# Attention block on one Trainium2 core: the first five and the last four tiles over two sets of buffers

## The chip, the cores and the metric

The kernel runs on one core of a Trainium2 chip. The core has TensorE (matrix products, its clock granted at one of two levels, 1.2 or 2.4 GHz), VectorE, ScalarE, GpSimd and SyncE, which here only issues DMAs. Each engine works through its own instruction list in order, and they meet through semaphores. The metric is the device time of one execution in microseconds; lower is better.

## The reference

An input `x` of 8 x 512 x 512 goes through three residual layers: half of an expert layer, a differential attention, and the expert layer again. Cut to what matters:

```python
x = x + 0.5 * ffn(layernorm(x))      # phase 1
x = x + attn(layernorm(x))           # phase 2
x = x + 0.5 * ffn(layernorm(x))      # norm and expert product: phase 2, the choice: phase 3

def attn(x):                         # S = E = 512, H = 16, KVH = 4, D = 32
    q, k, v = x @ Wq, x @ Wk, x @ Wv          # 2*H*D, 2*KVH*D, KVH*D columns
    q, k = rope(q), rope(k)                   # k, v repeated over 4 heads
    scores = softmax(causal(q @ k.T) / sqrt(D))        # two maps for each head
    diff = softmax(causal(scores[0] - lam * scores[1]))
    att = rmsnorm(diff @ v) * rms_w * (1 - LAM_INIT)
    return att @ Wo

def ffn(x):                          # 16 experts with the same weight, 256 tokens each
    S = softmax(x @ router_w + router_b)
    G, idx = top_k(S.T, 256)
    return scatter_add(idx, G * (x[idx] @ expert_w + expert_b))
```

## The kernel before

The 4096 rows are 32 tiles (`NT`) of 128 rows, four (`TB`) to a batch. Phase 1 (to about 188 us) writes the first layer's result `x1` to DRAM. Phase 2 is the attention with the norm and the expert product behind it. Phase 3 (from 1858.74 us) chooses tokens and adds the output.

In phase 2 a tile passes three steps. **Preparation**: load `xs`, `stats` and `normalise`, a split in a high and a low fp16 half (`high`, `low`), the turning of both (`turn_x`) and its copy to `xt` (`take_x`), three products with `wqkv` into PSUM (`project(0..2)`, 12 matmuls each), `rope` on VectorE, `rope_add` and `rope_low` on GpSimd, `rope_high` on ScalarE, a second turning (`turn_chunks`) and its copies to `turned` (`take_chunks`). SyncE then spreads `turned` into `qs` and `ks` with 12 + 12 DMAs (`stack`). **Attention**: eight pairs of query tiles and heads for each of the 32 steps `K`. **After-work**: squares and sums of each head, a root on GpSimd (`head_root`), norm, split, turning, product with `wo` (`product_o`), the sum with `x1`, norm, root (`root2`), split, turning, the router's product, the expert's product (`expert`, 13 matmuls), and the store of `x2` and `y2`.

`run_bodies` writes each engine's list. Inside `body` a table of 24 slots says which step of preparation (for tile K + 5, `AHEAD`) and of after-work (for tile K - 5, `BEHIND`) stands beside which step of attention. Five tiles must be prepared before step 0, and four tiles (28 to 31) are left after the last body; nothing of attention runs beside these. They run in two loops, one over `alone` and one over `closing`:

```python
    with eng.Fori(0, AHEAD) as tau:
        for f, next_tile in alone:
            f(tau + 1 if next_tile else tau)
```

In these loops each buffer exists once (`xs`, `rot`, `scratch`, `split`, `turned`; `an`, `at`, `x2`, `post_bank`), apart from some more PSUM banks in the first (`spread[0]`) and one other buffer in the second. SyncE's part of the first loop is

```python
                with sp.Fori(1, AHEAD) as u:
                    load(u + 1)
                    stack(u, None)
```

so the load of tile u + 1 stands behind the 24 DMAs of the stack of tile u - 1, which waits for that tile's last copy. The first product of attention, `energies`, waits for `turned_out` of tile 4 and for the stacks of tiles 0 to 3 to have landed. Below, the stretch from 188 us to that product is called the opening, the stretch from the last `weigh` to the first load of phase 3 the closing.

Of the kernel before, what the change touches and what calls it, by code (L numbers as in the profile page):

```python
# [15 lines left out]
ALU = mybir.AluOpType  # L16
# [7 lines left out]
ds = bass.ds  # L24
# [16 lines left out]
STEPS = 8  # L41
NC = (NQ + NK) // P
# [102 lines left out]
def run_bodies(eng, attention, side, ahead, alone, spread, closing):  # L145
# [10 lines left out]
    def body(K, tau, pi, pairs=True, more=True):  # L156
        known = {}
        for j in range(STEPS):
            for i in range(3):
# [4 lines left out]
                for f in side.get(3 * j + i, ()):  # L164
                    f(tau, pi)
# [4 lines left out]
    for slot in sorted(ahead):  # L170
        for f in ahead[slot]:
            f(0)
# [13 lines left out]
    body(NT, None, NT - BEHIND)  # L186
    spread[1] = True
    for f, next_tile in closing:
        if next_tile:
            f(NT - BEHIND + 1)  # L190
    with eng.Fori(NT - BEHIND + 1, NT - 1) as pi:
        for f, next_tile in closing:
            f(pi + 1 if next_tile else pi)
    for f, next_tile in closing:
        if not next_tile:
            f(NT - 1)
    spread[1] = False


def program(nc, x, wqkv, wo, we, wr, lams, rms, rb, eb, consts, out, x1_d, x2_d, y2_d):  # L200
# [14 lines left out]
    with top:  # L215
# [709 lines left out]
        with ExitStack() as ctx:  # L925
# [31 lines left out]
            ast = sb2("ast", [P, 4, H])  # L957
            an = sb2("an", [P, E])
# [9 lines left out]
            spread = [False, False]  # L968

            def project_bank(n):  # L970
                return bank[:, (4, 5, 0)[n] if spread[0] else 4, :]

            def chunk_pair(n):
                at = 1 + n if spread[0] else 4
                return bank[:, at, :].bitcast(F16).rearrange("p (a n) -> p a n", a=2)

            HEADS, ROWS = slice(0, E), slice(E, 2 * E)

# [27 lines left out]
            x2_st, y2_st = sem2("x2_st"), sem2("y2_st")  # L1006
            x1_t = x1_d.rearrange("b (t p) e -> (b t) p e", p=P)
# [6 lines left out]

            def last(f):

                return lambda pi: f(None, pi)
# [30 lines left out]
            def _(sp):  # L1048
# [13 lines left out]
                def stack(u, K):  # L1062
# [5 lines left out]
                    for dst, order, c0, c1, done in ((qs, (0, 1, 0), 0, CQ, stacked_q),  # L1068
                                                     (ks, (0, 0, 1), CQ, NC, stacked_k)):
                        to = dst[:, :, :].rearrange("p (r c i) (t s) -> p r c i t s", r=2, i=4, s=P)  # L1070
                        for j, part in enumerate(order):
                            for i in range(4):
                                sp.dma_start(to[j * D:(j + 1) * D, ds(ring, 1), :, i, ds(t, 1), :]
                                             .rearrange("p r c t s -> p (r c) (t s)"),
                                             turned[i * D:(i + 1) * D, part, c0:c1, :]).then_inc(done, 16)
# [8 lines left out]

                for g in range(2):
                    sp.wait_ge(x1_st[g], 16)
                load(0)
                load_again(0)
                load(1)
# [24 lines left out]
                with sp.Fori(NT - AHEAD, NT + BEHIND - 1) as K:  # L1114
                    finish(K, False, True, None)
                finish(NT + BEHIND - 1, False, False, None)
# [4 lines left out]
            def _(dve):  # L1121
# [84 lines left out]

                def rope(n):

                    width = 512 if n < 2 else NK
                    heads = width // (2 * D)  # L1210

                    def f(u, pi):
                        if u is None:
                            return
                        t = u & 3
# [3 lines left out]
                        src = project_bank(n)[:, 0:width]  # L1219
                        proj_done.wait(dve, 3 * u + n)  # L1220
                        rlo_done.wait(dve, 3 * u + n - 1)
                        cos = cst[:, ds(t * (2 * D) + C_COS, 2 * D)]
                        sin = cst[:, ds(t * (2 * D) + C_SIN, 2 * D)]
                        dve.tensor_tensor(rot[:, 0:width].rearrange("p (h f) -> p h f", h=heads),
                                          src.rearrange("p (h f) -> p h f", h=heads),
                                          cos.unsqueeze(1).broadcast_to([P, heads, 2 * D]), ALU.mult)

                        s4 = src.rearrange("p (h a r f) -> p h a r f", h=heads, a=2, r=2)
                        o4 = rot_t[:, 0:width].rearrange("p (h a r f) -> p h a r f", h=heads, a=2, r=2)
                        n4 = sin.rearrange("p (a r f) -> p a r f", a=2, r=2)  # L1230
                        for r in range(2):
                            for a in range(2):
                                ins = dve.tensor_tensor(  # L1233
                                    o4[:, :, a, r, :], s4[:, :, a, 1 - r, :],
                                    n4[:, a, r, :].unsqueeze(1).broadcast_to([P, heads, D // 2]), ALU.mult)
                        ins.then_inc(rope_v.sem, 1)
# [3 lines left out]
                def head_sums(u):  # L1240
                    sq_done.wait(dve, u)
                    sums_of = rot if spread[1] else asq
                    dve.tensor_reduce(ast[:, 0, :], sums_of[:, :].rearrange("p (h d) -> p h d", h=H), X, ALU.add)\
# [36 lines left out]
                def take_logits(u):  # L1280
# [3 lines left out]

                run_bodies(dve,
# [6 lines left out]
                           [(tile(rope(0)), 0), (stats, 1), (tile(rope(1)), 0), (normalise, 1), (tile(rope(2)), 0)], spread,  # L1292
                           [(add, 0), (normalise2, 0), (take_logits, 0), (head_sums, 1), (head_norm, 1)])

            @blk.gpsimd
            def _(gp):
# [42 lines left out]

                def rope_add(n):  # L1340
# [452 lines left out]
```

## Time and profile before

| | |
|---|---|
| median of 3 runs | 1957.39 us (1941.44, 1957.39, 1961.42) |
| profiled execution | 1944.41 us, its span 1942.3 us |
| granted TensorE clock, mean | 0.848 of 2.4 GHz |
| PE, DVE, ACT, POOL busy | 77%, 75%, 65%, 56% of the span |
| opening | 188.46 to 350.66 us |
| attention, 32 steps | 350.66 to 1761.87 us |
| closing | 1761.87 to 1858.74 us |
| phase 3 | 1858.74 us to the end |

The shares are means over stages that have little in common. In the opening and the closing each engine is idle most of the time, so there the order of events counts and not the sums. The idle time in front of an instruction and its releaser stand in square brackets in a timeline.

### The profile page before, as it was taken

Reading aid. Unit: us, or ns where it says so; the run is one execution under the profiler, and the core shown is the slowest. Engines: PE = TensorE matmul, PEld = TensorE weight load, DVE = VectorE, ACT = ScalarE, POOL = GpSimd, SP = SyncE. Lnnn points to the kernel's source line nnn. Section 1 sums busy time; section 2 is a strip of 40 time slices with the busy share of each in tenths; the row PEclk is TensorE's granted clock in tenths of the full one; section 3 lists DMA queues with packets and bytes.
Section 4 is the critical chain, followed back from the end, with each engine's and each line's share of the span. In section 5 each row is a group of like instructions: output and inputs, shape, how many; then the busy total and the mean of one; then the engine's idle time right before and its main releaser. Section 6 shows DMA issues by size and latency. Waiting matters only on the chain. (4 is left out here: it accounts for less than half of the span.)

```text
span 1942.3 us, 44349 instructions
## 1 busy us (share of the span) xinstructions
PE 1497.7 (77%) x10688; PEld 1038.7 (53%) x10688; DVE 1449.4 (75%) x5497; ACT 1258.2 (65%) x3422; POOL 1097.1 (56%) x1505
## 2 busy tenths in 40 slices
PE   3995434588888888998889988998889888885520
PEld 3542211366666666666666666666666666663210
DVE  6687211687889889898898889898898867751268
ACT  2361121687878888888888888887888877852120
POOL 5320222565677777677776777677777655652200
PEclk9997767688889989899999989899999778766655
DMA  7025111111111111121111111121111100001176
GB/s 288 3 81 184 31 35 42 26 38 33 28 32 54 42 42 47 46 53 45 44 53 42 47 42 47 46 53 44 44 53 41 40 16 22 16 17 33 38 268 259
DMA packets 179669, 117.25 MB, mean 60 GB/s; under 512 B 139169, under 2 KB 139553, under 8 KB 179618
## 3 DMA queue, kind: packets, MB, share of 16 engines
q1 hardware_dynamic: 179618, 116.65, 20.4%
q8 instruction: 22, 0.36, 0.1%
q14 instruction: 29, 0.24, 0.0%
HBM read 51.57 MB, written 33.55 MB: 44 GB/s over the span
## 5 line engine op out<-in xcount | busy, mean ns | idle before, releaser
L1415 ACT ACTIVATE ex<-bank,nbias 128x512 f32<-128x512 f32 (+3 forms) x1024 | 527.7, 538 | 67.5 <-DVE bank L1134 64.8
L1134 DVE TENSOR_SCALAR_CACHE_REDUCE bank<-bank,nesc 128x512 f32<-128x512 f32 (+3 forms) x1024 | 503.6, 553 | 61.9 <-PE bank L1561 60.8
L1591 PEld LDWEIGHTS bank<-vs,pr 128*128 128x128 f32 x2560 | 334.6, 206 | 23.2 <-issue 12.2
L1591 PE MATMUL bank<-vs,pr 128*128 (+1 forms) x2560 | 339.7, 284 | 8.6 <-issue 4.1
L1573 PE MATMUL bank<-cst,df 128*128 128x128 f32 x1280 | 264.5, 309 | 86.7 <-ACT pr L1432 85.9
L1314 POOL TENSOR_SCALAR ex<-ex,gam 128x128 f32<-128x128 f32 (+3 forms) x512 | 314.0, 624 | 0.0
L1559 PE MATMUL bank<-ks,qs 96*128 (+2 forms) x1024 | 262.1, 333 | 50.9 <-ACT ex L1415 48.7
L1432 ACT ACTIVATE pr<-bank 128x128 f32<-128x128 f32 (+3 forms) x512 | 231.7, 453 | 88.8 <-PE bank L1573 87.7
L1160 DVE CUSTOM_DVE_ANT_0 df<-ex 128x128 f32<-128x128 f32 (+3 forms) x512 | 258.9, 520 | 8.8 <-issue 4.5
L1573 PEld LDWEIGHTS bank<-cst,df 128*128 128x128 f32 x1280 | 168.0, 165 | 114.2 <-ACT pr L1432 98.3
L1415 ACT ACTIVATION_READ_ACCUMULATOR ex<-bank,nbias 128x1 f32 x1024 | 222.8, 218 | 0.0
L1561 PE MATMUL bank<-mask_b,ident_b 128*128 128x128 bf16 x1024 | 207.7, 237 | 0.0
L1424 ACT ACTIVATE df<-df,dbias,rsum 128x512 f32<-128x512 f32 (+1 forms) x256 | 201.6, 787 | 0.0
L1559 PEld LDWEIGHTS bank<-ks,qs 96*128 (+1 forms) x1024 | 109.7, 107 | 140.9 <-issue 73.3
L1346 POOL TENSOR_TENSOR rot<-rot,scratch 128x512 f32<-128x512 f32 (+1 forms) x96 | 105.1, 1095 | 123.8 <-DVE scratch L1233 123.8
L1321 POOL TENSOR_SCALAR df<-df,rsum,dbias 128x128 f32<-128x128 f32 (+1 forms) x256 | 149.9, 586 | 39.4 <-DVE dbias L1169 39.3
L1361 POOL TENSOR_TENSOR split<-rot,split 128x512 f16<-128x512 f32 (+1 forms) x96 | 95.3, 992 | 123.5 <-ACT split L1460 123.5
L247 PE MATMUL bank<-wqkv_h,b_xt 128*128 128x512 f16 (+1 forms) x384 | 156.2, 407 | 8.0 <-ACT b_xt L1484 5.9
L248 PE MATMUL bank<-wqkv_l,b_xt 128*128 128x512 f16 (+1 forms) x384 | 156.1, 406 | 0.0
L249 PE MATMUL bank<-wqkv_h,b_xt 128*128 128x512 f16 (+1 forms) x384 | 155.7, 406 | 0.0
L1134 DVE DVE_READ_ACCUMULATOR bank<-bank,nesc 128x1 f32 x1024 | 142.9, 140 | 0.0
L1148 DVE SCALAR_TENSOR_TENSOR gam<-esum,lam,rsum 128x2 f32<-128x2 f32 x256 | 115.2, 450 | 33.8 <-DVE rsum L1141 24.9
(279 smaller groups left out, 2958.5 us busy)
## 6 DMA issues: line engine op xcount, KB each, us to landing
qs<-turned SPq DMA_DIRECT2D x384, 64.0 KB, 2.1
x_dram<-xa SPq DMA_DIRECT2D x8, 1024.0 KB, 4.9
b_xs<-x_dram SPq DMA_DIRECT2D x32, 256.0 KB, 2.6
x<-x_dram SPq DMA_DIRECT2D x32, 256.0 KB, 2.6
x_dram<-x SPq DMA_DIRECT2D x32, 256.0 KB, 2.0
y_dram<-scratch SPq DMA_DIRECT2D x32, 256.0 KB, 2.0
c_x<-x_dram SPq DMA_DIRECT2D x8, 1024.0 KB, 14.5
c_y<-y_dram SPq DMA_DIRECT2D x8, 1024.0 KB, 15.0
```

The costliest lines, as they stand in the source:

```text
L247: eng.matmul(acc, a_hi(k), b_hi(k), start=first and k == 0, stop=False)
L248: eng.matmul(acc, a_hi(k), b_lo(k), start=False, stop=False)
L1134: dve.tensor_scalar(part, part, nesc[:, 0:1], None, ALU.mult, ALU.min, accum_out=nbias[:, j, i, a:a + 1]).then_inc(bias_done.sem, 1)
L1160: dve.tensor_tensor_reduce(out=df[j % 4][:, lo:hi], in0=ex[j % 4][:, 0, lo:hi], in1=ex[j % 4][:, 1, lo:hi], scale=1.0, scalar=-3e38, op0=A ...
L1314: gp.tensor_scalar(ex[j % 4][:, 1, lo:hi], ex[j % 4][:, 1, lo:hi], gam[:, j, i:i + 1], 1.0, ALU.mult, ALU.mult).then_inc(scaled.sem, 1)
L1415: ac.activation(ex[j % 4][:, a, lo:hi], energy(j, i)[:, a, :], ACT.Exp, bias=nbias[:, j, i, a:a + 1], scale=-1.0, accum_out=esum[:, j, i, ...
L1424: ac.activation(df[j % 4][:, lo:hi], df[j % 4][:, lo:hi], ACT.Identity, bias=dbias[:, j, 1:2], scale=rsum[:, j, 1, 0:1]).then_inc(shifted_ ...
L1432: ac.activation(pr[j % 2][:, lo:hi], bank[:, 6, 0:hi - lo], ACT.Exp).then_inc(prob_done.sem, 1)
L1559: pe.matmul(out_e, q.rearrange("p a n -> p (a n)"), k.rearrange("p a n -> p (a n)"), start=True, stop=True)
L1561: mm = pe.matmul(out_e[:, n - P:n], ident_b[:, :], mask_b[:, :], start=False, stop=True, skip_group_check=True)
L1573: tr = pe.transpose(bank[:, 6, k * P:(k + 1) * P], df[j % 4][:, lo + k * P:lo + (k + 1) * P], ident)
L1591: mm = pe.matmul(bank[:, 7, t * DV:(t + 1) * DV], pr[j % 2][:, lo + k * P:lo + (k + 1) * P], val, start=(k == 0), stop=(k == t))
```

## The change

Both loops are written out tile by tile, with every step of a tile over one of two sets of buffers (`u % 2` or `q % 2`; in the closing each of the four tiles has its own memory, and the PSUM banks alternate). The second set lies in memory that is not in use then: `att`, `ex`, `df`, `pr` in the opening, `qs` (by fp32 views) in the closing. Each engine has a `prologue` and a `closing` that fix the order in which it takes the tiles' steps. SyncE loads tiles 0 and 1 first, 2 and 3 before the first stack, 4 behind it, and `stack_first` waits for the stack before it to have landed. The last body ends at slot 12 for after-work, so that the norm, the router and the expert of tile 27 move into `closing`, behind the squares and sums of tile 28. In the closing the squares move from GpSimd to ScalarE and the low halves from GpSimd to VectorE. The arithmetic is the same.

```diff
-    spread[0] = True
-    with eng.Fori(0, AHEAD) as tau:
-        for f, next_tile in alone:
-            f(tau + 1 if next_tile else tau)
-    spread[0] = False
+    prologue()
     body(0, AHEAD, None)
...
-    body(NT, None, NT - BEHIND)
...
+    body(NT, None, NT - BEHIND, slots=DRAIN)
+    closing()
...
+                def load_first(u):
+                    if u >= 2:
+                        lo_done.wait(sp, u - 2)
+                    sp.dma_start(p_xs[u % 2], flat(x1_t[ds(u, 1), :, :])).then_inc(first_in[u], 16)
+
+                def stack_first(u):
+                    for done in (stacked_q, stacked_k):
+                        sp.wait_ge(done, u * 192 + 16)
+                    stack(u, None, p_turned[u % 2])
...
-                stack(0, None)
-                with sp.Fori(1, AHEAD) as u:
-                    load(u + 1)
-                    stack(u, None)
+                load_first(2)
+                load_first(3)
+                stack_first(0)
+                load_first(4)
+                stack_first(1)
+                load(AHEAD)
+                stack_first(2)
+                stack_first(3)
+                stack_first(4)
...
+                e_done.wait(sp, 2 * pair(NT - 1, STEPS - 1) + 1)
+                for q in range(CLOSE):
+                    sp.dma_start(c_x2(q), flat(x1_t[ds(LAST + q, 1), :, :])).then_inc(last_in[q], 16)
...
+                def first_chunks(u, n):
+                    c0, c1 = CHUNKS[n]
+                    rt_done.wait(ac, 3 * u + n)
+                    if u >= 2:
+                        ac.wait_ge(stacked_k if c0 >= CQ else stacked_q, (u - 1) * 192 + 16)
...
+                def prologue():
+                    first_turn(0)
+                    for u in range(AHEAD):
+                        first_project(u, 0)
+                        if u >= 1:
+                            first_chunks(u - 1, 1)
+                        first_project(u, 1)
+                        if u >= 1:
+                            first_chunks(u - 1, 2)
+                        if u + 1 < AHEAD:
+                            first_turn(u + 1)
+                        first_project(u, 2)
+                        first_chunks(u, 0)
...
+                def closing():
+                    turn_x2(LAST - 1)
+                    route(LAST - 1)
+                    expert(LAST - 1)
+                    prob_done.wait(pe, 2 * pair(NT - 1, STEPS - 1) + 1)
+                    att_out.wait(pe, (NT // TB) * H - 1)
+                    close_heads(0)
+                    close_o(0)
+                    close_heads(1)
+                    close_o(1)
+                    close_heads(2)
+                    close_o(2)
+                    close_turn2(0)
+                    close_expert(0)
+                    close_heads(3)
+                    close_o(3)
```

SyncE at the start of phase 2, before (`b_xs` is the tile loaded for preparation, `qs` and `ks` the stack, `x` the tile for the after-work; the loop begins at the branch):

```order
L1055 DMA b_xs<-x_dram 128x512
L1060 DMA x<-x_dram 128x512
L1055 DMA b_xs<-x_dram 128x512
L1073 DMA qs<-turned 32x8x128 x12
L1073 DMA ks<-turned 32x2x128 x12
L1094 UNCONDITIONAL_BRANCH
L1094 ISA
L1055 ISA
L1055 DMA b_xs<-x_dram 128x512
```

The same place now:

```order
L1138 DMA b_xs<-x_dram 128x512
L1138 DMA att<-x_dram 128x512
L1110 DMA x<-x_dram 128x512
L1138 DMA b_xs<-x_dram 128x512
L1138 DMA att<-x_dram 128x512
L1123 DMA qs<-turned 32x8x128 x12
L1123 DMA ks<-turned 32x2x128 x12
L1138 DMA b_xs<-x_dram 128x512
L1123 DMA qs<-ex 32x8x128 x12
L1123 DMA ks<-ex 32x2x128 x12
L1105 DMA b_xs<-x_dram 128x512
```

All five loads now stand ahead of the second stack, where before the third load stood behind the first stack and each later one behind a further stack.

ScalarE in the closing, before (L1489 and L1494 copy the two turned halves, L1478 and L1469 make the high halves of the second and the first norm, L1523 takes the expert's product; one pass of the loop is one tile):

```order
L1489 COPY at<-bank 128x1024
L1478 CAST split<-an 128x512
L1494 COPY at<-bank 128x1024
L83 REGISTER_ALU
L1469 CAST split<-an 128x512
L1522 ISA
L1523 COPY scratch<-bank 128x512
L191 REGISTER_ALU
L191 COMPARE_AND_BRANCH
```

ScalarE where the closing begins now (L1844 squares, L1849 and L1853 the heads' high half and the turned copy, L1738, L1754 and L1837 those of tile 27, L1857 the second norm's high half):

```order
L1844 ACTIVATE qs<-att 128x512 x4
L1738 CAST split<-an 128x512
L1754 COPY at<-bank 128x1024
L1849 CAST qs<-qs 128x512
L1853 COPY qs<-bank 128x1024
L1837 COPY scratch<-bank 128x512
L1849 CAST qs<-qs 128x512 x2
L1853 COPY qs<-bank 128x1024
L1849 CAST qs<-qs 128x512
L1857 CAST qs<-qs 128x512
L1853 COPY qs<-bank 128x1024
```

The steps of four tiles now stand between one another: two high halves of later tiles precede the copy that the next product of an earlier tile waits for.

## Rows read from the trace of the kernel before

**Rows 1.** Page, busy tenths of VectorE in 40 slices of 48.6 us.

```profile
DVE  6687211687889889898898889898898867751268
```

**Rows 2.** Windows: us; busy us (x) of PE, PEld, DVE, ACT, POOL; granted clock; DMA share.

```profile
320.00:336.00 16.00, 10.66 (x44) 4.58 (x44) 1.48 (x5) 0.99 (x2) 2.41 (x2) 0.81 0.27 56
188.00:351.00 163.00, 63.72 (x321) 31.58 (x322) 28.57 (x100) 29.86 (x46) 42.08 (x42) 0.66 0.18 43
1725.00:1762.00 37.00, 31.82 (x179) 24.21 (x177) 10.40 (x35) 14.10 (x26) 13.21 (x15) 0.68 0.07 22
1762.00:1859.00 97.00, 49.29 (x212) 20.10 (x212) 16.71 (x42) 15.28 (x20) 27.05 (x20) 0.66 0.10 33
```

**Rows 3.** Timeline of SyncE's queue: start us, us, engine, line, operation, out<-in, count.

```profile
220.04 8.00 SPq L1073 DMA_DIRECT2D qs<-turned  x12
228.08 8.17 SPq L1073 DMA_DIRECT2D ks<-turned  x12
...
303.23 0.35 SPq L1055 DMA_DIRECT2D b_xs<-x_dram  x1
317.96 8.82 SPq L1073 DMA_DIRECT2D qs<-turned  x12
326.98 8.77 SPq L1073 DMA_DIRECT2D ks<-turned  x12
336.40 0.35 SPq L1055 DMA_DIRECT2D b_xs<-x_dram  x1
351.16 9.55 SPq L1073 DMA_DIRECT2D qs<-turned  x12
```

**Rows 4.** Timeline, fourth tile to first attention product; in brackets idle before, releaser.

```profile
323.39 0.63 PE L248 MATMUL bank<-wqkv_l,b_xt 128*128 128x512 f16 x1
...
323.82 0.63 PE L249 MATMUL bank<-wqkv_h,b_xt 128*128 128x512 f16 x1
...
326.42 0.38 PE L247 MATMUL bank<-wqkv_h,b_xt 128*128 128x512 f16 x1
...
326.63 0.38 PE L248 MATMUL bank<-wqkv_l,b_xt 128*128 128x512 f16 x1
...
350.01 0.60 ACT L1502 COPY turned<-bank 128x512 f16<-128x512 f16 x1
...
350.66 0.61 PE L1559 MATMUL bank<-ks,qs 96*128 96x512 f16 x1 [1.47 <-ACT turned L1502]
```

**Rows 5.** Timeline of TensorE, last body and closing.

```profile
1756.18 0.61 PE L1679 MATMUL bank<-bias_b,ones_b 128*128 128x512 bf16 x1 [0.27 <-DVE logits L1282]
...
1760.67 1.20 PE L1591 MATMUL bank<-vs,pr 128*128 128x33 f32 x10
1770.06 1.03 PE L1605 MATMUL bank<-ident_h,split 128*128 128x128 f16 x8 [8.19 <-POOL split L1367]
```

**Rows 6.** Timeline of SyncE's queue: the last store, the next stage's first load.

```profile
1856.24 0.34 SPq L1083 DMA_DIRECT2D y_dram<-scratch  x1
1858.74 0.35 SPq L406 DMA_DIRECT2D d_csel<-in_consts  x1
```

**Rows 7.** Groups by form, closing: busy us, mean ns, idle us before, releaser.

```profile
L1390 POOL TENSOR_TENSOR ast<-ast,half 128x16 f32<-128x16 f32 x4 | 11.6, 2908 | 10.6 <-DVE ast L1250 10.6
...
L1372 POOL TENSOR_TENSOR split<-an,split 128x512 f16<-128x512 f32 x4 | 4.6, 1151 | 5.2 <-ACT split L1478 5.2
...
L1494 ACT COPY at<-bank 128x1024 f16<-128x1024 f16 x4 | 4.0, 1012 | 9.7 <-PE bank L1605 9.7
...
L1256 DVE TENSOR_TENSOR an<-att,ast 128x512 f32<-128x512 f32 x4 | 2.8, 693 | 12.4 <-POOL ast L1390 12.4
```

**Rows 8.** DMA issues by line: KB each, median us from issue to landing.

```profile
qs<-turned SPq DMA_DIRECT2D x384, 64.0 KB, 2.1
...
ks<-turned SPq DMA_DIRECT2D x384, 16.0 KB, 1.8
```

**Rows 9.** Timeline of GpSimd where the last body begins.

```profile
1728.17 1.27 POOL L1384 TENSOR_TENSOR scratch<-att 128x512 f32<-128x512 f32 x1 [2.01 <-issue]
```

More of the change, by code:

```diff
@@ L41 @@
 STEPS = 8
+DRAIN = 12
+CLOSE = BEHIND - 1
 NC = (NQ + NK) // P
@@ L142, with run_bodies, body @@
     v_ring = property(lambda self: self._get("v_ring", lambda K: (K >> 2) % VR))
-def run_bodies(eng, attention, side, ahead, alone, spread, closing):
-    def body(K, tau, pi, pairs=True, more=True):
+def run_bodies(eng, attention, side, ahead, prologue, closing):
+    def body(K, tau, pi, pairs=True, more=True, slots=3 * STEPS):
         known = {}
@@ L1397, in _ @@
                            {18: [root], 21: [low]},
-                           [(rope_add(0), 0), (rope_low(0), 0), (root, 1), (rope_add(1), 0), (rope_low(1), 0), (rope_add(2), 0),
-                            (rope_low(2), 0), (low, 1)], spread,
-                           [(root2, 0), (low2, 0), (last(square), 1), (head_root, 1), (low_heads, 1)])
+                           prologue,
+                           closing)
             @blk.scalar
@@ new lines, in first_project, with first_chunks @@
+                def first_project(u, n):
+                    width = 512 if n < 2 else NK + NV
+                    xt_out.wait(pe, u)
+                    if u >= 2:
+                        rope_v.wait(pe, 3 * (u - 2) + n)
+                        if n == 2:
+                            v_done.wait(pe, u - 2)
+                    three(pe, p_bank(u, n)[:, 0:width], *parts(p_xt[u % 2], wqkv_h, wqkv_l, n * 512, n * 512 + width))\
+                        .then_inc(proj_done.sem, 1)
+                def first_chunks(u, n):
+                    c0, c1 = CHUNKS[n]
+                    rlo_done.wait(pe, 3 * u + n)
+                    if n == 0 and u >= 1:
+                        turned_out.wait(pe, 3 * (u - 1) + 2)
+                    elif n == 1:
+                        xt_out.wait(pe, min(u + 1, AHEAD - 1))
+                    elif n == 2:
+                        turned_out.wait(pe, 3 * u)
+                    for a in range(2):
+                        for c in range(c0, c1):
+                            tr = pe.transpose(p_pair(P_C[n])[:, a, (c - c0) * P:(c - c0 + 1) * P],
+                                              p_split[u % 2][:, a, c * P:(c + 1) * P], ident_h[:, :])
+                    tr.then_inc(rt_done.sem, 1)
@@ new lines, in close_expert @@
+                def close_expert(q):
+                    xt2_out.wait(pe, LAST + q)
+                    three(pe, c_bank(2, q)[:, 0:NX], *parts(c_xt2(q), wr_h, wr_l, 0, NX)).then_inc(route_done.sem, 1)
+                    if q >= 2:
+                        y_out.wait(pe, LAST + q - 2)
+                    pe.matmul(c_bank(3, q), ones_b[:, :], bias_b[:, :], start=True, stop=False)
+                    three(pe, c_bank(3, q), *parts(c_xt2(q), we_h, we_l, 0, E), first=False).then_inc(y_done.sem, 1)
```

463 lines of the change are left out of this document (394 added, 69 removed).

## The prediction, written before the changed kernel was run

> **What bounds the kernel now.** I read the page's slices first: VectorE is busy for six to nine tenths of most of them, but for one or two in slices 5 to 7 and 37 and 38 [rows 1]. Windows give the sizes: in the opening, 163 us, TensorE is busy 63.7 us, GpSimd 42.1 and the others less; in the closing, 97 us, TensorE 49.3 us and the others at most 27 [rows 2]. So in both stretches no engine is the bound; order is.
>
> Opening: SyncE's timeline shows it [rows 3]. Tile 4's load goes out at 336.40, behind the stack that began at 317.96; the load before it was at 303.23. That is a period of 33.2 us, made of about 18 us of stack issue (8.82 + 8.77 and a gap) and 15 us in which the next tile is finished while SyncE waits. The two stand in series because the load of the next tile is queued behind the stack, and its last PSUM reads wait for that load's statistics on VectorE. The first product of attention starts at 350.66, released by the last copy of tile 4 [rows 4]; the stack of tile 3 had been issued by 335.75.
>
> Closing: TensorE ends its last attention product at 1761.87 and then idles 8.19 us for tile 28's halves [rows 5]. The last `y2` store goes out at 1856.24 and phase 3 starts at 1858.74 [rows 6]. That is 97 us for four tiles, 24 us each, a chain of short steps, the longest the 2.91 us root on GpSimd [rows 7].
>
> **The opening, worked out.** What is removed is the series: loads 2 to 4 no longer wait for a stack. What stays is the issue of the stacks. Written out without register work, the first one takes 8.00 + 8.17 us and a small gap, 16.2 us for 24 DMAs [rows 3]; in the loop it was 17.8. Added is a wait in `stack_first` for the stack before: the last DMA lands 1.8 us after its issue begins [rows 8], and one issue is 0.68, so SyncE goes on 1.2 us behind the end of it, hand-over included. So SyncE's period is 16.2 + 1.2, 17.4 us, and 17.5 with the two loads in between. Behind that wait only loads are queued that nobody needs yet, and the copies of tiles 2 to 4 into the shared buffer, which wait for a stack two tiles back.
>
> Does the compute keep up? TensorE needs for a tile 12 matmuls of each width. At the low level two of 512 columns start 0.43 us apart (323.39, 323.82), at the high one 0.21 (326.42, 326.63) [rows 4]; 384 columns take three quarters of that. So 36 matmuls are 14.1 us low and 7.1 high, and the turnings add 3.6 or 2.2: 17.7 or 9.3 us. GpSimd was busy 42.1 us in the opening's five tiles, 8.4 each, VectorE and ScalarE about 6 each [rows 2]. At the high level SyncE is the bound, at the low level TensorE ties with it and the copies that wait on each other come on top. I followed both through the lists with these durations and 0.1 us for each hand-over. High level: the first stack starts at 217.4, the fourth has landed at 217.4 + 3 x 17.5 + 17.4, 287.3. Low level: the tiles are ready 17.8 us apart from 229, the fourth at 282.3, landed at 299.9. Before, this stretch was granted 0.66 on the mean, and 0.81 where the projections run without a pause [rows 2]. Now TensorE works in longer runs with pauses of 1 to 5 us; I take a level of 0.78, a first stack at about 221, and a landing at 291.5. Tile 4 is turned earlier than that in either case. The gain is 350.66 - 291.5, **59 us**, with ends of 51 and 63.
>
> Here a rule speaks against the sum. The rows show 16.2 us to issue what lands in 1.8 to 2.1 us each [rows 3, 8], so SyncE's issue sets the stack's time. The Trainium skill, in DMA: Bandwidth & Descriptors, section Issuing engines are not separate DMA queues, says that the sequencer's time to start a DMA is usually small against the DMA itself. By that rule the stack would cost little and attention would wait for tile 4 alone, at 270 to 292; the trace does not agree with it here, and the row decides.
>
> **The attention.** Its 32 steps take 1761.87 - 350.66, 1411 us, and none of their instructions changes. Stack 4 started 0.5 us behind the first product before (351.16) and starts with it now, so the first steps meet the same SyncE list. I cost this at nothing; if the stack of a later tile were late, SyncE's list would show it before the fifth step.
>
> **The closing, worked out.** First, the last body loses tile 27's turning, router and expert. The expert alone held TensorE from 1756.18 to 1760.67 ahead of the last attention product [rows 5]; with 0.6 and 0.4 us for the other two and their waits it is 6.3 us, so that product ends near 1755.5. Then comes a lead-in: squares 0.6 (ScalarE's copy of the same size [rows 4]), sums of an estimated 1.1 (0.7 for a VectorE pass over 512 columns, as in L1256, and two small ones), root 2.91 [rows 7], then tile 27's low half 1.15 (queued behind that root on GpSimd), turning 1.0, copy 1.0, tile 28's high and low half 1.3, logits 0.2 and ten hand-overs: 10.3 us until `expert(27)` starts. That expert is 13 matmuls, 5.7 us low or 2.9 high. Per tile TensorE then has 12 + 13 matmuls of 512 columns, two turnings and the router: 13.5 us low, 7.4 high, 54 or 29.5 for four. The copies of the turned halves take 1.01 us [rows 7], with hand-overs 1.2 us of waiting at each of eight, since nothing else of TensorE's stands between a turning and its product: 9.4 us (10.7 high, where ScalarE is now and then late). The last copy, the store and the end take 3.1. Low: 1755.5 + 10.3 + 5.7 + 54 + 9.4 + 3.1 = 1838. High: 1754.5 + 10 + 2.9 + 29.5 + 10.7 + 3.1 = 1811. The root, 2.91 us a tile, and the subtractions, which leave GpSimd at 1.15 us for VectorE at 0.7 (its multiplication of the same size) [rows 7], now lie beside TensorE's work; if that cover were gone they would cost 4 us a tile.
>
> The level decides between the ends. The closing was granted 0.66 [rows 2] while TensorE idled in pauses of up to 8.2 us, and in runs of 5 us of matmuls; in the opening a run that was still low at 323.82, was high at 326.42 [rows 4], so the closing's runs end about where their level would rise. Now pauses are 1 to 2.5 us. I take 0.78, between this row and the 0.81 of the unbroken projections: 1823. The gain is 1858.7 - 1823, **36 us**, with ends of 21 and 48.
>
> A second rule bears on both places: the Trainium skill, TensorE: Matmul & The Clock Gate, part 1, says that the throttled level is the default and sustained activity releases it. By it the denser lists would run at the high level throughout, a rival below.
>
> **Sum.** 59 + 36 = 95 us. Against its own profiled execution: 1944.4 - 95 = 1849. That execution is 13 us under the median of the three runs, which I keep as the offset: **1862 us**, a ratio of 0.951.
>
> **The rivals.** (a) TensorE stays at the high level in both stretches: 63 + 48 = 111, 1846 us. For it: 0.81 in the projections; against: 0.68 even from 1725 to 1762, where TensorE was busy 31.8 of 37 us [rows 2]. (b) It stays low: 51 + 21 = 72, 1885 us. For it: the closing of before; against: the shorter pauses. (c) The in-order lists tangle in the closing, above all ScalarE's, where high halves of later tiles stand ahead of the copy that TensorE waits for. If each tile costs 6 us more, three fifths of the gain there goes: 1862 + 24 = 1886. (d) Attention gives the head start back, because the first steps wait for `stack(5)` and later ones: 59 us less, up to 1921. Against it: a step lasts 1411 / 32, 44 us, and a stack 18. (e) Issue does not bind the stacks and attention waits only for tile 4: with compute near 280, 12 us better, 1850. (f) Slower: the long straight lists must be fetched as they run. The last body began on GpSimd with 2.01 us in which it waited for nothing but issue [rows 9]. To eat 95 us, 47 such pauses would have to lie on the path; TensorE's list grows by a tenth, so I see four or five, 10 us. From 57 pauses on the kernel would be slower by over 1%, 1977 us. (g) Nothing moves, because something else, such as the stores of `x1`, holds the first stack: 1957 us.
>
> **How the numbers follow.** The forecast 0.60, (a) 0.10, (b) 0.12, (c) 0.07, (d) 0.04, (e) 0.04, (f) 0.01, (g) 0.02. The range reaches from (a), less the offset of a fast run, to (b): 1840 to 1886. It leaves out (d), (f), (g) and parts of (a) to (c). A measurement of this kernel tells about 1% from no change; faster by more than that is all but (f) and (g), 0.97.
>
> **What would show it.** Right: stacks in SyncE's timeline 17 to 18 us apart; the first `energies` product near 291, released by the landing of the fourth stack and no longer by a copy; the steps of attention as long as before; the last `weigh` near 1696 with 67 us from there to phase 3; TensorE's waits in the closing about 1.2 us each and its granted clock near 0.78. Wrong: stacks 20 us or more apart (TensorE or a wait for landing sets them), waits of 3 us and more on ScalarE's copies, or a longer attention stage.

## The result, and the profile after

The kernel after takes **1840.97 us** (median of 4 runs, 1828.35 to 1847.27), the kernel before, run beside it, 1949.41 us (4 runs, 1939.53 to 1961.42). The ratio is **0.9461** with a 95% interval of 0.941 to 0.9512, a gain of 108 us where 95 had been forecast. The profiled execution took 1838.54 us, its span is 1836.7, so the spans differ by 105.6 us.

First the page of the kernel after, VectorE's tenths and the granted clock in slices of 45.9 us.

```profile
DVE  5778425888889898898889988898989877674477
...
PEclk9998776788899899999999899998999887676855
```

VectorE's gap in front of the attention has shrunk to two slices, and the two slices behind it, at one and two tenths before, are at four [rows 1]. The same view by windows, with the columns of [rows 2], over the opening, the attention and the closing of the kernel after:

```profile
188.50:288.00 99.50, 49.89 (x320) 26.80 (x321) 28.36 (x100) 29.61 (x46) 40.68 (x42) 0.76 0.29 73
288.00:1696.50 1408.50, 1245.76 (x9067) 908.59 (x9067) 1193.48 (x4754) 1127.09 (x3195) 967.65 (x1377) 0.88 0.16 41
1696.50:1753.20 56.70, 35.08 (x245) 17.73 (x245) 22.87 (x51) 18.89 (x27) 15.97 (x9) 0.86 0.11 42
```

The opening fell from 162.2 us to 99.5, the attention from 1411.2 to 1408.5, the closing from 96.9 to 56.7: 62.7 + 2.7 + 40.2 is the whole difference of the spans. Phases 1 and 3 stayed as they were.

**Opening.** The timeline of SyncE's queue, then of TensorE and ScalarE where the attention starts:

```profile
219.24 8.41 SPq L1123 DMA_DIRECT2D qs<-turned  x12
227.70 8.24 SPq L1123 DMA_DIRECT2D ks<-turned  x12
235.98 0.58 SPq L1138 DMA_DIRECT2D b_xs<-x_dram  x1
237.21 7.79 SPq L1123 DMA_DIRECT2D qs<-ex  x12
...
254.15 7.80 SPq L1123 DMA_DIRECT2D qs<-turned  x12
261.99 7.75 SPq L1123 DMA_DIRECT2D ks<-turned  x12
271.00 7.79 SPq L1123 DMA_DIRECT2D qs<-ex  x12
278.83 7.75 SPq L1123 DMA_DIRECT2D ks<-ex  x12
287.84 8.44 SPq L1123 DMA_DIRECT2D qs<-turned  x12
```

```profile
263.54 1.93 ACT L1796 COPY turned<-bank 128x1024 f16<-128x1024 f16 x2 [4.60 <-DMA qs<-turned]
271.00 0.58 ACT L1796 COPY turned<-bank 128x512 f16<-128x512 f16 x1 [5.54 <-DMA ks<-turned]
...
288.01 0.59 PE L1928 MATMUL bank<-ks,qs 96*128 96x512 f16 x1 [22.73 <-DMA ks<-ex]
```

A stack is the 24 DMAs of one tile, `qs` and then `ks`. The stacks begin 18.0, 16.9 and 16.9 us apart where they were 33.2 [rows 3], with at most 1.3 us between the last issue of one and the first of the next. Tile 4's last copy is done at 271.6, but TensorE waits until 288.01 for the landing of the fourth stack; before, a copy released it [rows 4].

**Closing.** The timeline of TensorE, with GpSimd's two steps in front of tile 27's turning, and the store and load at the end:

```profile
1693.66 2.82 PE L1960 MATMUL bank<-vs,pr 128*128 128x33 f32 x20
...
1698.65 3.17 POOL L1636 TENSOR_TENSOR rot<-rot,half 128x16 f32<-128x16 f32 x1 [7.11 <-DVE rot L1417]
1701.80 1.17 POOL L1616 TENSOR_TENSOR split<-an,split 128x512 f16<-128x512 f32 x1
...
1703.12 1.01 PE L1974 MATMUL bank<-ident_h,split 128*128 128x128 f16 x8 [6.64 <-POOL split L1616]
...
1706.96 0.63 PE L232 MATMUL bank<-we_h,at 128*128 128x512 f16 x1
...
1712.08 0.75 PE L2098 MATMUL bank<-ident_h,qs 128*128 128x128 f16 x8
1713.94 0.39 PE L232 MATMUL bank<-wo_h,qs 128*128 128x512 f16 x1 [1.10 <-ACT qs L1853]
...
1740.95 10.09 SPq L1192 DMA_DIRECT2D y_dram<-qs  x3
1753.17 0.34 SPq L391 DMA_DIRECT2D d_csel<-in_consts  x1
```

And TensorE's waits in the closing (engine, line waited for, us in total, times, longest):

```profile
PE bank L1974 <- POOL split L1616: 6.6, 1, 6.6
PE bank L232 <- ACT qs L1853: 5.3, 4, 2.0
PE bank L232 <- ACT qs L1861: 4.6, 4, 1.2
```

Tile 28's turning starts 15.6 us behind the end of the last `weigh`; from there to the copy of the last `y` at 1750.08 it is 38 us, with TensorE waiting only for the copies of its own turnings, some 1.2 us each. Of the long waits on GpSimd [rows 5] one of 6.64 us is left. The product of 512 columns shows 0.63 us in tile 27's expert and 0.39 from tile 28's output product on.

### The profile page after: what moved, and what is told of

Read it like the earlier page. It is cut to its first block and busy times, and to the rows that moved or that the text cites. A ratio compares the mean times of both kernels' runs of the same rounds, so it can differ in the third digit from the quotient of the medians.

```text
span 1836.7 us, 43825 instructions
## 1 busy us (share of the span) xinstructions
PE 1473.0 (80%) x10688; PEld 1035.1 (56%) x10688; DVE 1456.8 (79%) x5505; ACT 1260.1 (69%) x3426; POOL 1082.6 (59%) x1493
## 5 line engine op out<-in xcount | busy, mean ns | idle before, releaser
L1928 PE MATMUL bank<-ks,qs 96*128 (+2 forms) x1024 | 266.2, 337 | 68.7 <-ACT ex L1675 45.4
L1605 POOL TENSOR_TENSOR split<-rot,split 128x512 f16<-128x512 f32 (+1 forms) x81 | 80.4, 993 | 111.3 <-ACT split L1720 111.3
L232 PE MATMUL bank<-wqkv_h,b_xt 128*128 128x512 f16 x360 | 142.3, 395 | 3.2 <-ACT turned L1762 1.2
L234 PE MATMUL bank<-wqkv_h,b_xt 128*128 128x512 f16 x360 | 142.9, 397 | 0.0
L233 PE MATMUL bank<-wqkv_l,b_xt 128*128 128x512 f16 x360 | 142.2, 395 | 0.0
L1515 POOL TENSOR_SCALAR_AFFINE_SELECT ex<-ex 128x256 f32<-128x256 f32 x256 | 120.9, 472 | 22.2 <-DVE gam L1234 22.2
```

The costliest lines, as they stand in the source:

```text
L234: mm = eng.matmul(acc, a_lo(k), b_hi(k), start=False, stop=last and k == KT - 1)
L1928: pe.matmul(out_e, q.rearrange("p a n -> p (a n)"), k.rearrange("p a n -> p (a n)"), start=True, stop=True)
```

## The experiments

All stretches below run from 188.5 us to the first `energies` product (opening) and from the last copy of heads, which follows the last `weigh`, to the first load of phase 3 (closing). Kernels that ran once are read by their stretches; their whole times are given, but the attention between differs by up to 15 us from one profiled execution to another (last section).

**Each half alone.** The closing of before under the opening of after, and the reverse:

```diff
-    body(NT, None, NT - BEHIND, slots=DRAIN)
-    closing()
+    body(NT, None, NT - BEHIND)
...
+    with eng.Fori(NT - BEHIND + 1, NT - 1) as pi:
+        for f, next_tile in closing:
+            f(pi + 1 if next_tile else pi)
```
```diff
-    prologue()
...
+    with eng.Fori(0, AHEAD) as tau:
+        for f, next_tile in prologue:
+            f(tau + 1 if next_tile else tau)
```

> The opening of the kernel after with the closing of the kernel before (phase 2's full last body, its loop over tiles 28 to 31, one set of buffers). Theory: the two parts of the change add up. The first energies product then stands at about 288 us of the span and the stretch from the last weigh product to the first load of phase 3 at about 97 us again; the time is some 63 us below the kernel before (ratio about 0.968) and 43 above the kernel after. Rival: part of the 63 us is given back in the attention or depends on the new closing; then the ratio is 0.98 or more, or the attention from the first energies to the last weigh product takes more than 1412 us.

> The opening of the kernel before (its loop over five tiles) with the closing of the kernel after. Theory: the first energies product stays at about 351 us, the closing takes 55 to 59 us in place of 97, and the time is some 40 to 43 us below the kernel before (ratio about 0.979). Rival: the closing's gain came with a TensorE that ran at another level through the whole execution; then the closing takes 65 us or more here and the ratio is 0.985 or more.

Measured: 1875.09 us for the opening alone, ratio 0.9669 (0.9643 to 0.9695), and 1889.66 us for the closing alone, 0.974 (0.972 to 0.976). The windows: the opening and the closing of the first kernel, and the closing of the second.

```profile
188.50:288.60 100.10, 51.24 (x320) 27.72 (x321) 28.38 (x100) 29.51 (x46) 40.61 (x42) 0.72 0.28 71
```
```profile
1691.40:1788.40 97.00, 47.81 (x208) 20.14 (x212) 16.69 (x41) 15.27 (x20) 27.06 (x20) 0.65 0.10 33
```
```profile
1749.10:1805.50 56.40, 34.17 (x242) 17.59 (x245) 22.86 (x51) 18.89 (x27) 15.97 (x9) 0.86 0.11 43
```

Both rivals fall: the stretches are those of the whole change, 100.1 and 56.4 us, and neither half needs the other. The product of the two ratios is 0.942, inside the interval of the whole change. The opening is as long, to 0.6 us, at a clock of 0.72 as at 0.76, so a difference of that size in the clock does not set it.

**What binds the opening.** Three kernels. In the first each stack counts its landings on semaphores of its own, so that SyncE need not wait:

```diff
 def stack_first(u):
-    for done in (stacked_q, stacked_k):
-        sp.wait_ge(done, u * 192 + 16)
-    stack(u, None, p_turned[u % 2])
+    stack(u, None, p_turned[u % 2], (last_in[u], first_in[u]) if u < TB else None)
```

The second only swaps two lines (`load_first(4)` ahead of `stack_first(0)`). The third does both and has ScalarE issue a part, where `stack_piece(engine, tile, keys, thirds)` is the part of `stack` for queries or keys alone:

```diff
                         first_rope_high(u, 2)
+                        if u == AHEAD - 1:
+                            stack_piece(ac, 3, False)
                         first_chunks(u, 0)
+                        if u == 2:
+                            stack_piece(ac, 1, True)
                     first_chunks(AHEAD - 1, 1)
+                    stack_piece(ac, 3, True, (2,))
                     first_chunks(AHEAD - 1, 2)
```

> The kernel after, where SyncE issues a stack of the opening without waiting for the landing of the one before (each of tiles 0 to 3 counts its landings on semaphores of its own, and the common ones are raised when all four have landed). Theory: SyncE's 24 issues set the distance of the stacks, 15.4 to 15.6 us of the 16.9; only the 1.3 us between the last issue and the next first one goes, so the stacks stand 15.5 us apart and the first energies product comes at 283 to 285 us in place of 288. Rival: the landing wait is the bound and the issues queue up behind transfers; then the stacks stay 16.8 us apart, or the landing comes later after the issue than 2.5 us.

> The kernel after with tile 4's load issued ahead of the first stack in SyncE's list. Theory: computation is not what the attention waits for; tile 4 is ready some 9 us earlier, SyncE's stacks begin 0.5 to 0.8 us later, and the first energies product comes at 288 to 289 us. Rival (the last of the opening that I gave a chance): the wait of tile 4 for its load is what costs; then the first energies product comes 5 to 9 us earlier, at 279 to 283 us.

> The kernel after with semaphores of their own for the stacks of tiles 0 to 3, tile 4's load ahead of the first stack, and a part of the stacks issued by ScalarE: the keys of tile 1, the queries and a third of the keys of tile 3 (28 of the 96 transfers that the first energies product needs). Theory: the time from the first stack to the first energies product is issue time on SyncE (0.65 us each), so taking 28 of 96 off it brings the first energies product to 267 to 272 us, 16 to 21 us earlier, and the time to a ratio of about 0.990 against the kernel after (0.937 against before). Rival (the rule that the sequencer's time to start a transfer is small and the queues share the same engines): the transfers are the bound; then the first energies product does not come before 283 us.

Measured: the first `energies` product came at 284.3 without the landing wait (1837.06 us), at 286.8 with the early load (1836.97 us), and at **267.2** over two queues (1815.62 us, ratio to before 0.9331, 0.9264 to 0.9398). A part of each gain is only where the first stack began: at 217.55, 217.65 and 215.92, for 219.24 in the kernel after. In the two kernels with fillers and with added columns below, whose openings are those of the kernel after, it began at 218.00 and 217.80, so nearly 2 us of this differ between executions of the same list. From the first stack to the `energies` product it is 68.8 us in the kernel after, 66.7 without the landing wait, 69.2 with the early load and 51.3 over two queues.

So the early load let tile 4's first product begin 10.0 us sooner (238.40 for 248.37) and gained nothing, since its copies wait for a stack's landing (5.54 us in both) and the attention for the fourth stack; that 286.8 lies below the 288 to 289 expected is the earlier first stack. Without the landing wait the result lies in the range, but only by that start, and not by the spacing I expected: the stacks stood 17.0, 16.9 and 15.7 us apart, not 15.5, since two loads of 0.5 us stand between them and single halves took 8.0 to 8.35 us. The wait is worth 2.1 us. Over two queues, without that wait and with 28 of 96 DMAs on ScalarE, it is 17.5 us. The timeline of SyncE's queue, then of ScalarE:

```profile
215.92 7.99 SPq L1105 DMA_DIRECT2D qs<-turned  x12
224.35 8.70 SPq L1105 DMA_DIRECT2D ks<-turned  x12
233.09 8.10 SPq L1105 DMA_DIRECT2D qs<-ex  x12
...
241.92 7.94 SPq L1105 DMA_DIRECT2D qs<-turned  x12
249.91 7.99 SPq L1105 DMA_DIRECT2D ks<-turned  x12
257.95 5.24 SPq L1105 DMA_DIRECT2D ks<-ex  x8
```
```profile
229.32 8.27 ACTq L1105 DMA_DIRECT2D ks<-ex  x11
...
255.00 7.91 ACTq L1105 DMA_DIRECT2D qs<-ex  x12
263.01 1.01 ACT L1816 COPY turned<-bank 128x1024 f16<-128x1024 f16 x1 [7.61 <-issue]
```

ScalarE issues 12 DMAs in 7.91 us while SyncE issues 12 in 7.99, and both keep that pace side by side. So the time belongs to the issuing engine and not to what the two share. It is some 0.65 us for a DMA, and its price is that ScalarE does nothing else meanwhile (7.61 us in which it waited for issue). By the rule of the Trainium skill that the prediction weighed (DMA: Bandwidth & Descriptors, section Issuing engines are not separate DMA queues), starting a DMA is usually small against the DMA itself; the runs do not agree with it here, where the issue is 0.65 us and the landing comes some 2 us after it began.

**Order or buffers, and the level.** One kernel keeps the closing's buffers, banks and instructions, and puts every engine's list in the order of one tile after another:

```diff
-                    close_heads(0)
-                    close_o(0)
-                    close_heads(1)
...
+                    for q in range(CLOSE):
+                        close_heads(q)
+                        close_o(q)
+                        close_turn2(q)
+                        close_expert(q)
```

Two others put extra products in TensorE's waits of the closing of before (under the opening of after):

```diff
+def fill(n):
+    for _ in range(n if SPREAD[1] else 0):
+        pe.matmul(bank[:, 0, :], ident_h[:, :], wo_h[:, 0, :], start=True, stop=True)
```

> The kernel after with its closing's buffers, banks and instructions kept, but each engine's list for the last four tiles in the order of one tile after another, as the loop of the kernel before had it (only the squares, roots and norm of the next tile beside the expert of this one). Theory: what gains is the order, since a tile's chain of waits is what sets a tile's time; the closing then takes 84 to 92 us of the 97 before, at a granted clock near 0.67, and the time is 27 to 35 us above the kernel after. Rival: the own buffers, the squares on ScalarE and the low parts on VectorE are what gains; then the closing takes 57 to 65 us.

> The kernel of the run with the opening alone, whose closing is that of before, with extra products of 128x512 in TensorE's waits of the closing (22, 4, 6, 4 and 1 for each of four tiles, into a bank that nothing reads; they add work and change no result). Theory: TensorE's level accounts for about half of the closing's 40 us. With the waits filled it runs at the high level, 25 products of a tile take 0.216 us each in place of 0.427, and the closing takes 72 to 80 us in place of 97 at a clock above 0.9. Rival: the level is worth little there, because the other engines' steps set the time, or the fillers themselves stand in the way; then the closing takes 90 us or more.

> As the run with fillers before it, with their numbers after the waits that they are to fill: 14 before a tile's first turning (wait 1.4 us, 4 with a faster expert product), 22 before its second (wait 5.5 us), the rest as it was. Theory: the order of one tile after another makes the level worth little: tile by tile 12 output products and two turnings gain 3.3 us, the expert's do not, since the next tile's turning waits for its low part 6.8 us after the logits in either case; the closing takes 82 to 86 us in place of 97. Rival, as I had it first: all 25 products gain; then it takes 72 to 80. A second rival: fillers cost what they give, and it takes 90 or more again.

Measured: one tile after another, the closing takes 88.2 us at a clock of 0.72 (1863.59 us). With the first numbers of fillers it takes 92.7 at 0.89 (1867.58 us), with the others 85.4 at 0.98 (1862.24 us). The windows of the closing, one tile after another and with the second set of fillers:

```profile
1690.10:1778.30 88.20, 47.06 (x240) 20.64 (x245) 22.67 (x51) 19.52 (x27) 14.98 (x9) 0.72 0.07 27
```
```profile
1691.40:1776.80 85.40, 69.06 (x388) 31.35 (x390) 16.63 (x41) 15.08 (x20) 27.06 (x20) 0.98 0.11 37
```

The first filler run failed my expectation and came out as its rival, and I had been wrong twice. I had set the large number before the shorter wait: 22 products ran to 1721.0 in front of a turning whose low part was ready at 1718.7. And I had counted all 25 products of a tile as gain. The timelines show why they are not, first of the closing before (in the run with the opening alone), then with fillers placed:

```profile
1715.06 0.69 DVE L1361 TENSOR_REDUCE ast<-rot 128x16 f32<-128x512 f32 x1
1716.20 2.91 POOL L1630 TENSOR_TENSOR ast<-ast,half 128x16 f32<-128x16 f32 x1 [3.13 <-DVE ast L1368]
...
1721.87 0.62 PE L1972 MATMUL bank<-ident_h,split 128*128 128x128 f16 x8 [1.36 <-POOL split L1607]
```
```profile
1713.06 0.69 DVE L1361 TENSOR_REDUCE ast<-rot 128x16 f32<-128x512 f32 x1
1714.20 2.91 POOL L1630 TENSOR_TENSOR ast<-ast,half 128x16 f32<-128x16 f32 x1 [2.70 <-DVE ast L1368]
...
1719.86 0.62 PE L1972 MATMUL bank<-ident_h,split 128*128 128x128 f16 x8 [0.68 <-POOL split L1607]
```

From the sums to the next tile's turning it is 6.8 us in both, however fast TensorE does the expert product beside it. So in the order of before the high level gave 11.6 us of 97, by fillers that may themselves have cost something.

For the order, 88.2 and 97.0 do not compare the same work: one tile after another, tile 27's turning, router and expert stand behind the last `weigh`, where the closing of before has them in the last body. The attention's list is the same in the three kernels up to the first exponential (ScalarE's `ex<-bank`) of its last step. Counted from there to phase 3, with the opening alone, then one tile after another, then in the kernel after:

```profile
1616.30:1788.40 172.10, 111.02 (x596) 69.02 (x601) 56.81 (x204) 58.68 (x135) 63.52 (x69) 0.68 0.08 26
```
```profile
1622.60:1778.30 155.70, 104.53 (x596) 66.41 (x601) 61.83 (x212) 60.92 (x139) 50.51 (x57) 0.73 0.08 29
```
```profile
1628.00:1753.20 125.20, 94.33 (x603) 64.07 (x602) 62.24 (x213) 60.45 (x140) 51.24 (x57) 0.78 0.10 36
```

The own buffers and the moved steps, tile 27's end among them, gave 16.4 us of 47, and the order 30.5, the higher level that it brings included. In the order of one tile after another TensorE still waits 4.6 us a tile for the second norm's halves (18.3 us in all), where it was 5.4 before (21.6 in all).

**Tile 27 ahead of tile 28.**

On VectorE `normalise2(27)` moves from behind `close_sums(0)` into the last body, ahead of the last copy of heads. On ScalarE and GpSimd:

```diff
-                    for q in range(CLOSE):
-                        close_square(q)
                     high2(None, LAST - 1)
+                    close_square(0)
                     take_x2(LAST - 1)
+                    close_square(1)
+                    close_square(2)
+                    close_square(3)
```
```diff
-                    close_root(0)
                     low2(LAST - 1)
+                    close_root(0)
```

> The kernel after with tile 27's end moved ahead of tile 28's beginning: VectorE's norm of tile 27 stands ahead of its last copy of heads, ScalarE casts it ahead of the squares, GpSimd takes its low part ahead of tile 28's root. Theory: TensorE waits 6.6 us in front of tile 27's turning for nothing but this order; the turning follows the last weigh product at once, tile 27's expert product ends when tile 28's turning is ready, and the closing takes 49 to 51 us in place of 56.7 (ratio about 0.996 against the kernel after). Rival: tile 28's chain of squares, sum, root (3.2 us), norm, high and low part is late anyhow, so TensorE waits there instead; then the closing takes 54 us or more.

Measured: 1822.2 us, ratio to before 0.937 (0.9298 to 0.9442); the closing takes 49.3 us. The timeline:

```profile
1686.66 1.04 PE L1977 MATMUL bank<-ident_h,split 128*128 128x128 f16 x8
...
1689.57 0.61 PE L2095 MATMUL bank<-bias_b,ones_b 128*128 128x512 bf16 x1 [0.27 <-DVE logits L1406]
...
1695.09 0.79 PE L2101 MATMUL bank<-ident_h,qs 128*128 128x128 f16 x8
```

Tile 27's turning follows the last `weigh` without a wait, and tile 28's low part is ready when the expert product ends. The span is 16.9 us shorter than that of the kernel after; 7.4 us of it are the edit's own, 10.2 lie in the attention up to the last `weigh`, where the edit moves one norm on VectorE and nothing of TensorE's (the opening is 0.6 us longer).

**Both edits that gained.**

> The kernel after with both edits that gained alone: the opening's stacks over two queues (20.8 us in its opening) and tile 27's end moved ahead of tile 28's beginning (7.4 us in its closing). Theory: they lie in different stretches and add up to 28 us; the first energies product comes at 267 us, the closing takes 49 to 50 us, and the ratio to the kernel before is 0.925 to 0.933. Rival: one stretch takes back what the other gives, as the attention's last bodies seem to do from run to run (their TensorE level differed between the kernels so far by 14 us for the same instructions); then the ratio is 0.934 or more.

Measured: **1809.8 us** (6 runs, 1806.22 to 1819.57), ratio to before **0.9301** (0.9278 to 0.9324), a better kernel than both. The first `energies` product comes at 268.8, the closing takes 48.6 us at a clock of 0.95. They add up: 19.2 + 8.1 us in the stretches, 27.9 between the spans of the kernel after and of this one.

**Columns in the last bodies.** This one is about the attention's level (last section).

```diff
+def fill(tau, pi):
+    if tau is None and not (isinstance(pi, int) and pi >= NT - BEHIND):
+        for _ in range(6):
+            pe.matmul(bank[:, 4, :], ident_h[:, :], wo_h[:, 0, :], start=True, stop=True)
```

> The kernel after with 18 extra products of 128x512 in each of the attention's bodies 27 to 31, which have no projections any more (into a bank that nothing reads; added work). In these bodies the granted clock is 0.6 to 0.8 although TensorE is busy 88% of the time, and they take 40 to 45 us, no less than the ones before them that have 36 such products more at 0.95. Theory: it is the missing wide products that let the level fall; with 18 of them back (3.9 us each body at the high level) the clock there is above 0.85 and a body takes 36 to 39 us, 12 to 25 us less in all. Rival: the level does not follow from that; then the bodies get longer by the fillers' 4 to 8 us each, 15 to 35 in all.

Measured: 1833.74 us. The windows over the same 180 us ahead of the last body, of the kernel after and of this one:

```profile
1496.50:1676.50 180.00, 156.66 (x965) 119.66 (x964) 127.72 (x550) 129.04 (x378) 103.03 (x151) 0.72 0.07 23
```
```profile
1491.70:1671.70 180.00, 154.57 (x1081) 110.10 (x1084) 132.99 (x568) 134.07 (x392) 105.03 (x155) 0.88 0.07 25
```

The clock rose from 0.72 to 0.88 as the theory has it, and a body took 39.7 to 43.5 us in place of 40.0 to 45.6. That is far from the 36 to 39 expected. Five bodies, from tile 22's second norm on VectorE to tile 27's, took 206.7 us with the added columns and 214.8 in the kernel after, but 204.8 in the run with tile 27 ahead, which has no added columns and a clock of 0.78 there. So the fillers give back what they cost, and the attention as a whole, 1405.1 us, is no shorter than it is from one execution to another. The theory is right in that the added products raise the level, and wrong on the worth; whether it is their columns or the mere pauses that they fill was not tested apart.

## Why the prediction was right, and where it was off

**What bounds the kernel: right.** Order bound both stretches. Each half alone gave its own stretch, and everything but the order gave 16.4 of the closing's 47 us. One row was misread: the load at 336.40 is tile 5's, and tile 4's is the one at 303.23 [rows 3]. VectorE's timeline before shows how tile 5's held tile 4: its statistics stand ahead of the reads of tile 4's products.

```profile
339.13 0.69 DVE L1195 BATCH_NORM_STATS2 norms<-b_xs 128x6 f32<-128x512 f32 x1 [11.59 <-DMA b_xs<-x_dram]
...
340.35 0.69 DVE L1224 TENSOR_TENSOR rot<-bank,cst 128x512 f32<-128x512 f32 x1
```

The period of 33.2 us and its two parts in series stand all the same.

**Opening, 59 us: measured 62.7.** The step that SyncE's issue sets the distance of the stacks held, and two queues show it. Between my 291.5 and the measured 288.0, 1.8 us are that the first stack began at 219.24 and not 221. Another 1.1 are that four stacks took 68.8 us and not 69.9: the first one's halves took 8.4 and 8.2 us, more than the 8.0 and 8.17 on which I had built [rows 3], the others 7.7 to 7.8. And 0.6 us are my own rounding, for 221 + 52.5 + 17.4 is 290.9. The level on which I had let the first stack depend mattered little; my calculation at the high level said 287.3, the trace says 288.0 at a clock of 0.76, with a later start and shorter stacks that nearly cancel.

**Attention at nothing: right, as far as can be told.** It was 1408.5 us; I had 1404.9 (1411.2 less the 6.3 us of tile 27's end). The last step, from its first exponential to the end of the last `weigh`, fell from 75.3 us to 68.4, 6.8 us where I took off 6.3, and the steps before it took 4.1 us longer with the same instructions. That is within what they took in the other runs. No stack was late, rival (d) is out. That the last `weigh` ended at 1696.5, where I had 1696, is two errors that cancel: the attention began 3.5 us sooner and took 3.6 longer.

**Closing, 36 us: measured 42.9** (2.7 in the attention's window, 40.2 behind it), or 47.0 without the attention's 4.1. The lead-in was right: 10.1 us to `expert(27)` for 10.3. The end was right, 3.1 us. The expert took 5.5 us, the low value. The term that was mis-sized is that of the four tiles with their copies: I took some 50 us at a level of 0.78, and they took 38, at a clock of 0.99 from 1712 to 1740, which is near the sum for the high level, 40.2. The reason that I gave for 0.78 was the level of the unbroken projections, 0.81 [rows 2]; but that window held the change of level itself, as [rows 4] showed. What the closing before at 0.66 had in it was waits of 5.4 us in each tile; with waits of 1.2 us the level did not fall again. So rival (a) was half right: high in the closing once it had risen, without any effect in the opening. The closing shows 0.63 us for each product of tile 27's expert, behind 10 us with little work, and 0.39 from the next tile on; with that the rule of the Trainium skill, TensorE: Matmul & The Clock Gate, part 1, that the low level is the default and activity releases it, agrees.

**The rivals.** (c) The in-order lists tangled only once, 2.0 us before one output product (my price for it was off as well: 24 of 36 us are two thirds, not three fifths). (e) falls with the early load: tile 4's products began sooner, and the attention did not. (b), (f) and (g) did not occur.

**The sum.** I forecast 1862 us and it is 1841. Half of the 21 us is the terms: 95 against 105.6 in the profiled executions, 1849 against 1838.5. The other half is the offset: I carried over 13 us from three runs of before, and it is 2.4 us for the kernel after (1840.97 - 1838.54), while four runs of before put its own at 5.0. A profiled execution that lies low among three runs says little about where the next one lies, and the middle of the range should have stood some 10 us lower for it. That the result still lies in the range has luck in it: 1840.97 is 1 us above its lower end of 1840, two of the four runs, 1828.35 and 1838.54, lie below, and it is nearer to rival (a), 1846, to which I gave 0.10, than to the forecast with 0.60.

## What to carry to other kernels

Where no engine is busy for much more than half of a stretch, write down for each engine what stands ahead of the step that all wait for: the closing's order was worth 30.5 us here, and a higher level in the old order 11.6. After such a change ask again what the last wait is: here one issuing engine's 96 DMAs, and one tile's end behind the next tile's beginning, were worth 28 us more. A faster TensorE is worth only what lies on the chain: with the level raised by fillers to 0.98, the old order still took 85 of its 97 us.

## What the runs showed of the hardware

**Issuing costs the issuing engine, and adds up over engines.** 12 DMAs of the stack held SyncE for 7.8 to 8.7 us and ScalarE for 7.9, at the same time, and each landed 1.8 to 2.2 us behind its issue (medians by line).

**The attention's level has more than one rhythm.** The attention's instructions up to the last body are the same in all kernels but the one with added columns. In those whose last body also leaves out tile 27's end it took 1397.4 to 1412.7 us, at 0.89 or 0.88. Between the kernel after (1408.5) and the run with tile 27 ahead (1398.2) nearly all of the difference lies in the last bodies, in which no projection stands: 180 us at 0.72 in the kernel after, and at 0.78 in the run with tile 27 ahead, whose window is this:

```profile
1486.90:1666.90 180.00, 154.25 (x1033) 120.28 (x1033) 133.42 (x573) 135.86 (x399) 107.50 (x159) 0.78 0.07 25
```

The four runs of the kernel after differ in the same way: 1828.35 us at a mean clock of 0.872, 1838.54 at 0.863, 1843.39 and 1847.27 at 0.861. TensorE is busy for 86 or 87% of these windows, and yet the level is at one time 0.72 and at another 0.78; with 18 products of 512 columns more in each body it rose to 0.88. What chooses the rhythm stays open.
